# Row maxima and scores of an ALiBi attention: the block bias with its operands swapped, the value matmuls spread evenly, one copy moved from GpSimd to ScalarE

## The chip, the cores and the metric

The kernel runs on one core of one Trainium2 chip. The metric is the device time of one execution in microseconds (us). Three runs of the kernel before gave 3437.27, 3439.45 and 3440.22 us, a median of 3439.45 us.

## What is computed

Four layers run one after another on 8 sequences of 1024 tokens by 256 channels, each as `x = x + layer(layernorm(x))`: a recurrent mixer, a feed-forward layer, attention, and the feed-forward layer again. Only the attention is touched. Its core is:

```python
qkv = (x @ Wqkv + bqkv).reshape(B, L, 3, 16, 16)         # B 8, L 1024
scores = jnp.einsum('bqhd,bkhd->bhqk', q, k) / math.sqrt(16)
bias = -jnp.abs(pos[None, :] - pos[:, None])
scores = scores + slopes[None, :, None, None] * bias[None, None]
probs = jax.nn.softmax(scores, axis=-1)
out = jnp.einsum('bhqk,bkhd->bqhd', probs, v).reshape(B, L, D)
return out @ Wout + bout
```

## The kernel before

The 16 heads of a batch are taken in 4 groups of 4, so attention has 32 groups, numbered 0 to 31. Query and key of a head are stacked in 64 partitions (`q_stack`, `k_stack`): high and low halves of the numbers, and rows that carry the linear part of the ALiBi bias and the shift of the softmax. TensorE's array is used in two row groups of 64, so that two heads' matmuls can run side by side.

A matmul over a stack gives 128 by 512 scores. The stacked rows describe the bias of a block of 128 by 128 on the diagonal only up to a correction. `add_block_bias` adds that correction to the 128 columns of such a block, by two matmuls in bfloat16 that accumulate in PSUM (L1537). Before, a table is the stationary operand (64 partitions by 128 columns) and a 64 by 64 identity, `unit`, is the moving one, so each of the two writes 64 columns.

Scores are computed twice. Once with queries on the partitions, by `find_maxima` (L1593): VectorE reduces each 128 by 512 result to row maxima (L1811), which are transposed on TensorE (L1584), copied by ScalarE (L1723), split by GpSimd into a high part (a copy that rounds, L1903) and the rest (L1905), and taken by DMA through DRAM into a row of `q_stack` (L1988, L1992). And once with keys on the partitions, by `attend` (L1654): ScalarE exponentiates 128 by 1024 scores of two heads (L1762) and TensorE weighs the values with them (`weigh`, L1609), in one PSUM bank that collects 8 key blocks. At the end of 8, ScalarE copies that bank out (L1731, semaphore `pv_made`), the first weighing of the next 8 waits for that copy, and `conclude` transposes the copy (L1621) for VectorE to normalize. For the last group of a batch, `conclude` also has 8 steps of output projection (L1632 to L1641), then the store of the batch and the load of a later one (L2007, L1951).

The order is written out, the same on each engine. A group has two halves (of 512 queries), a half has 8 key blocks `kb`, and a key block has 2 steps, `pair` 0 and 1. A **step** here is one such pair: two `attend` matmuls (one per row group), two `find_maxima` matmuls of the next group or the one after, and a weighing. So a group has 32 steps, attention 1024. In half of the steps the `attend` scores meet the diagonal, in half the maxima do, independently: of 32 steps, 8 have no block bias (plain), 16 have four of its matmuls, and 8 have eight. Row maxima run 80 of their turns ahead (the lead). They use a ring of three PSUM banks, `misc`, which all other short results share. `follow` says which weighing stands at a step's end, and calls `step()`, which takes `conclude` one step further. Other work is laid between by `side_by_side`: queries and keys for a later group (two blocks of 4 matmuls, near steps 2 and 7), values in the last group of a batch, LayerNorm in the second (`normalize`, whose bn_stats is L1782).

Of the kernel before, what the change touches and what calls it, by code (L numbers as in the profile page):

```python
# [7 lines left out]
BF16 = mybir.dt.bfloat16  # L8
# [3 lines left out]
ACT = mybir.ActivationFunctionType  # L12
AX = mybir.AxisListType

P = 128
# [25 lines left out]
GROUPS = HEADS // GROUP  # L41
QB = SEQ // P
# [4 lines left out]
STACK = SHIFTROW + 2  # L47
ROWGROUPS = P // STACK
# [8 lines left out]
def constants():  # L57
    c = {"c_ident": np.eye(P, dtype=np.float32)}

    s, t = np.arange(P)[:, None] % BLOCK, np.arange(BLOCK)[None, :]
    parts = [(s == t) | (s // 2 == t // 2) & (s % 2 == 0) & (t % 2 == 1)]
    for level in range(1, NEARBY):
        m = 1 << level
        parts.append(((s // (2 * m) == t // (2 * m)) & (s // m % 2 == 0))[:, t[0] // m % 2 == 1])
    c["c_mask"] = np.concatenate(parts, 1).astype(np.float32)

    q, power = np.arange(SEQ), np.asarray([power for _, power in slopes()])[:, None, None]
    picked = (q[None, :] // P == np.arange(QB)[:, None]).astype(np.float32)
    i, j = np.arange(QB)[:, None], q[None, :] // P
    sign, near = np.where(i == j, np.where(i < CT, -1, 1), np.sign(i - j)), np.arange(P)
    c["c_qrows"] = np.concatenate([(picked * (q % P))[1:QB - 1], picked])
    c["c_krows"] = np.ones((STACK - SHIFTROW, SEQ))
    c["c_kbias"] = np.concatenate([-power * sign[1:QB - 1], power * (sign * (q % P) - P * np.abs(i - j))], 1)
    short = np.minimum(0, 2 * (near[None, :] - near[:, None]))  # L80
    short = np.stack([short, short.T]).reshape(2, P // STACK, STACK, P)
    by_head = power[:, :, :, None, None] * short
    c["c_block"] = by_head.reshape(GROUPS, ROWGROUPS, GROUP // ROWGROUPS, 2, P // STACK, STACK, P).transpose(
        1, 5, 0, 2, 3, 4, 6).reshape(P, HEADS // ROWGROUPS, 2, P // STACK, P)
    c["c_unit"] = np.tile(np.eye(STACK), (ROWGROUPS, 1))
    c["c_qkscale"] = np.concatenate([np.repeat([HD ** -0.5 / unit for unit, _ in slopes()[:GROUP]], HD),
                                     np.ones(GROUP * HD)])[:, None]
    c = {k: v.astype(np.float32) for k, v in c.items()}
    return {k: np.ascontiguousarray(v) for k, v in c.items()}
# [1292 lines left out]
def attention(nc, banks, x_in, x_out, d):  # L1382
    with nc.cleanup_on_exit(), ExitStack() as ctx:
        sb = lambda n, s, dt=F32: ctx.enter_context(nc.sbuf_tensor("b_" + n, s, dt))
# [6 lines left out]
        PAIRS = GROUP // ROWGROUPS  # L1391
        PARTS = P // STACK
        WIDTH = BANK // 2

        ident, unit = sb("ident", [P, P]), sb("unit", [P, STACK], BF16)
        tables = sb("tables", [P, HEADS // ROWGROUPS, 2, PARTS, P], BF16)
        w_qk = sb("w_qk", [P, KT, GROUPS, 2 * GW])
        w_v, w_out = sb("w_v", [P, KT, DIM]), sb("w_out", [P, KT, DIM])
# [16 lines left out]
        shift, shift_full = sb("shift", [2 * GROUP * QB, P], F32R), sb("shift_full", [2 * GROUP * QB, P])  # L1415
# [14 lines left out]
        ident_in, weights_in, bias_cast, tables_cast = sem("ident_in"), sem("weights_in"), sem("bias_cast"), sem("tables_cast")  # L1430
# [3 lines left out]
        shift_out, shift_in = sem("shift_out"), [sem(f"shift_in{i}") for i in range(2)]  # L1434
# [8 lines left out]
        shift_hi, shift_copied, shift_made = sem("shift_hi"), sem("shift_copied"), sem("shift_made")  # L1443
# [44 lines left out]
        def tails(weigh, conclude):  # L1488

            waiting = []

            def values_of(t, part):
                if t >= 0:
                    use, kb = divmod(t, QB)
                    weigh(t, use, kb, part)
                    if kb == QB - 1 and part:
                        waiting.append(conclude(use // HALVES, use % HALVES))

            def step():
                if waiting and next(waiting[0], waiting) is waiting:
                    waiting.pop(0)

            def follow(t, pair):
                if pair == 0:
                    if (t - 2) % QB == 0:
                        values_of(t - 2, 0)
                    values_of(t - 2, 1)
                elif (t - 1) % QB:  # L1510
                    values_of(t - 1, 0)
                    step()

            def finish():
                end = ALL * HALVES * QB
                values_of(end - 2, 1)
                values_of(end - 1, 0)
                values_of(end - 1, 1)
                while waiting:
                    step()  # L1520

            return follow, finish
# [7 lines left out]

        def tensor(pe):
            def add_block_bias(out, g, pair, rg, variant):

                rows = slice(rg * STACK, (rg + 1) * STACK)
                for part in range(PARTS):
                    cols = slice(part * STACK, (part + 1) * STACK)
                    last = pe.matmul(out[:, cols], tables[rows, g % GROUPS * PAIRS + pair, 1 - variant, part, :], unit[rows, :],  # L1537
                                     start=False, stop=part == PARTS - 1, tile_position=(rg * STACK, 0))
                return last

# [136 lines left out]
        def scalar(act):  # L1677
# [38 lines left out]
            def find_maxima():  # L1716
                for g, turn, *_ in row_turns():
                    if g and turn == TURN + 1:
                        m = misc.at["turn", g - 1][0:2 * GROUP * QB, 0:P]
                        act.wait_ge(max_turned, g)  # L1720
                        if g >= 2:
                            act.wait_ge(shift_made, g - 1)
                        act.activation(shift_full[:, :], m, ACT.Copy).then_inc(shift_copied, 1)  # L1723
                    yield

# [133 lines left out]
        def gpsimd(pool):  # L1859
# [36 lines left out]
            def find_maxima():  # L1896
                lo = slice(0, GROUP * QB)
                for g, turn, *_ in row_turns():
                    if g and turn == TURN + 1:
                        pool.wait_ge(shift_copied, g)  # L1900
                        if g >= 2:
                            pool.wait_ge(shift_out, 16 * (g - 1))
                        pool.tensor_copy(shift[:, :], shift_full[:, :]).then_inc(shift_hi, 1)  # L1903
                        pool.wait_ge(shift_hi, g)
                        pool.tensor_tensor(shift[lo, :], shift_full[lo, :], shift[lo, :].bitcast(F32), ALU.subtract).then_inc(shift_made, 1)  # L1905
                    yield

# [27 lines left out]
            for first in range(0, P, STACK):  # L1935
                pool.dma_start(q_stack[first + MAIN:first + SHIFTROW, :, :], every_slot(d["c_qrows"])).then_inc(tables_cast, 16)
                pool.dma_start(k_stack[first + SHIFTROW:first + STACK, :, :], every_slot(d["c_krows"])).then_inc(tables_cast, 16)
            pool.dma_start(unit[:, :], d["c_unit"]).then_inc(tables_cast, 16)
            pool.dma_start(tables[:, :, :, :, :], d["c_block"]).then_inc(tables_cast, 16)
            pool.wait_ge(half_set, 1)  # L1940
            pool.wait_ge(bias_made, 1)
# [143 lines left out]
```

## Time and profile before

| | |
|---|---|
| median of three runs | 3439.45 us |
| the profiled execution | 3439.45 us, its span 3437.7 us |
| TensorE matmul / weight load, busy in the span | 3188.2 us (93%) / 1915.5 us (56%) |
| VectorE / ScalarE / GpSimd, busy | 2472.0 / 1989.0 / 779.2 us |
| block bias matmuls (L1537) | 4096, mean 197 ns |
| `attend` (L1654) / `find_maxima` (L1593) matmuls | 2048, mean 470 ns / 2048, mean 480 ns |
| row maxima on VectorE (L1811) | 2048, mean 686 ns |
| exponentials on ScalarE (L1762) | 1024, mean 1027 ns |

The 1024 steps take 1766.5 us, from 1289.57 to 3056.1 us of the span; in front of them stand the attention's own beginning and the lead. A length that the profile gives for a matmul includes its way through the array, so two that follow each other overlap in it; what a matmul costs is read from starts. `out<-in` names the tiles, and `x16` after a row of the timeline says that so many instructions were put together. A matmul on f32 appears as two instructions.

### The profile page before, as it was taken

To read this page: it belongs to the slowest core of one execution; us is meant where nothing else is said; L and a number is where in the kernel's file an instruction comes from. 1 tells how busy PE (TensorE), PEld (TensorE's weight loads), DVE (VectorE), ACT (ScalarE), POOL (GpSimd) and SP (SyncE) were. 2 spreads that over 40 slices of the span, in tenths; PEclk is the share of its full clock that TensorE was granted. 3 is DMA by queue.
4 is the path that set the end of the run, shared out by engine and by line. 5 is a ranking of instruction groups with operands and counts; after the bars stand their busy time and mean duration, and the time that the engine had idled before them with its cause. 6 is when DMAs were issued, how large, how long until landed. Compare 5 with 4: busy or idle time off the path is not lost. (4 is left out here: it accounts for less than half of the span.)

```text
span 3437.7 us, 77976 instructions
## 1 busy us (share of the span) xinstructions
PE 3188.2 (93%) x31396; PEld 1915.5 (56%) x31396; DVE 2472.0 (72%) x4742; ACT 1989.0 (58%) x2967; POOL 779.2 (23%) x920
## 2 busy tenths in 40 slices
PE   7999999977999479999999999999999999979998
PEld 3666666655777334454444544544445445437777
DVE  6877777737777258877778777787787777817776
ACT  3544445534555207666667666666676676765555
POOL 3444444432222201011021020110201201012222
PEclk9999999977999759999999999999999999989999
DMA  1000000002111322122222131222221312111110
GB/s 52 15 26 27 26 21 27 20 28 93 50 50 38 90 43 38 31 44 48 44 48 44 24 68 24 44 49 45 47 45 26 66 30 39 36 57 51 53 53 32
DMA packets 110295, 145.44 MB, mean 42 GB/s; under 512 B 21744, under 2 KB 94208, under 8 KB 109152
## 3 DMA queue, kind: packets, MB, share of 16 engines
q1 hardware_dynamic: 109168, 137.69, 17.1%
q8 instruction: 249, 4.08, 0.5%
q0 software_dynamic: 768, 2.77, 0.4%
q14 instruction: 110, 0.90, 0.1%
HBM read 53.79 MB, written 38.24 MB: 27 GB/s over the span
## 5 line engine op out<-in xcount | busy, mean ns | idle before, releaser
L1811 DVE TENSOR_REDUCE b_half_max<-banks 128x1 f32<-128x512 f32 x2048 | 1310.1, 686 | 423.2 <-PE banks L1537 273.1
L1762 ACT ACTIVATE b_p_t<-banks 128x1024 f32<-128x1024 f32 x1024 | 1040.7, 1027 | 366.5 <-PE banks L1537 234.5
L1593 PE MATMUL banks<-b_k_stack,b_q_stack 62*128 62x512 f32 x2048 | 827.6, 480 | 43.5 <-issue 17.8
L1654 PE MATMUL banks<-b_q_stack,b_k_stack 64*128 64x512 f32 x2048 | 833.2, 470 | 8.1 <-ACT b_p_t L1762 8.0
L1609 PE MATMUL banks<-b_p_t,b_v 128*17 128x256 f32 x8192 | 631.8, 386 | 0.2 <-ACT b_p_t L1762 0.2
L1654 PEld LDWEIGHTS banks<-b_q_stack,b_k_stack 64*128 64x128 f32 x2048 | 345.4, 186 | 421.9 <-issue 371.5
L1593 PEld LDWEIGHTS banks<-b_k_stack,b_q_stack 62*128 62x128 f32 x2048 | 339.2, 189 | 91.2 <-DVE b_half_max L1811 41.7
L1537 PE MATMUL banks<-b_unit,b_tables 64*128 64x64 bf16 x4096 | 371.3, 197 | 0.0
L1137 ACT ACTIVATE ffn_relu<-banks,ffn_scale_fc 128x512 f32<-128x512 f32 x256 | 176.2, 688 | 234.0 <-PE banks L1069 234.0
L1082 PE MATMUL banks<-ffn_proj_t,ffn_r_hi 128*128 128x256 f32 x1024 | 262.1, 289 | 9.0 <-DVE ffn_r_lo L1263 9.0
L1083 PE MATMUL banks<-ffn_proj_t,ffn_r_lo 128*128 128x256 f32 x1024 | 253.4, 280 | 0.0
L1537 PEld LDWEIGHTS banks<-b_unit,b_tables 64*128 64x128 bf16 x4096 | 185.2, 97 | 121.2 <-issue 73.1
L1609 PEld LDWEIGHTS banks<-b_p_t,b_v 128*17 128x17 f32 x8192 | 142.9, 95 | 173.2 <-ACT b_p_t L1762 50.7
L1261 DVE CAST ffn_r_hi<-ffn_square 128x512 fp32r<-128x512 f32 x256 | 129.2, 505 | 142.3 <-ACT ffn_square L1141 140.6
L1893 POOL TENSOR_TENSOR b_qk_lo<-b_qk,b_qk_hi 128x512 fp32r<-128x512 f32 x64 | 81.8, 1278 | 628.9 <-ACT b_qk L1712 474.2
L1082 PEld LDWEIGHTS banks<-ffn_proj_t,ffn_r_hi 128*128 128x128 f32 x1024 | 194.5, 190 | 24.6 <-DVE ffn_r_lo L1263 15.1
L1065 PE MATMUL banks<-ffn_x_hi,ffn_fc_t 128*128 128x512 f32 x512 | 203.3, 397 | 0.0
L1066 PE MATMUL banks<-ffn_x_lo,ffn_fc_t 128*128 128x512 f32 x512 | 202.7, 396 | 0.0
L1319 POOL TENSOR_TENSOR ffn_x<-ffn_x,ffn_scaled_out 128x256 f32<-128x256 f32 x128 | 108.2, 845 | 402.8 <-DVE ffn_scaled_out L1274 402.8
L1083 PEld LDWEIGHTS banks<-ffn_proj_t,ffn_r_lo 128*128 128x128 f32 x1024 | 193.4, 189 | 8.3
L1263 DVE TENSOR_TENSOR ffn_r_lo<-ffn_square,ffn_r_hi 128x512 fp32r<-128x512 f32 x256 | 177.3, 693 | 8.8
L1141 ACT ACTIVATE ffn_square<-ffn_relu 128x512 f32<-128x512 f32 x256 | 162.0, 633 | 8.2
(232 smaller groups left out, 4722.6 us busy)
## 6 DMA issues: line engine op xcount, KB each, us to landing
ffn_x<-x SPq DMA_DIRECT2D x32, 512.0 KB, 3.8
b_q_stack<-b_qk_hi SPq DMA_DIRECT2D x256, 64.0 KB
b_k_stack<-b_qk_hi SPq DMA_DIRECT2D x256, 64.0 KB
a_x<-hidden_states SPq DMA_DIRECT2D x16, 512.0 KB, 4.1
x<-a_x SPq DMA_DIRECT2D x16, 512.0 KB, 2.9
x<-ffn_x SPq DMA_DIRECT2D x16, 512.0 KB, 2.8
b_x<-x SPq DMA_DIRECT2D x8, 1024.0 KB, 5.5
b_k_stack<-b_qk_lo SPq DMA_DIRECT2D x128, 64.0 KB
```

Of the source, the lines that this page charges most:

```text
L1065: pe.matmul(b, fc_t[:, kt, cols], x_hi[:, kt, :], start=kt == 0, stop=False)
L1066: pe.matmul(b, fc_t[:, kt, cols], x_lo[:, kt, :], start=False, stop=False)
L1082: pe.matmul(b[:, 0:DIM], r_hi[par][:, m, i * P:(i + 1) * P], proj_t[:, m, :], start=m == 0, stop=False)
L1083: last = pe.matmul(b[:, 0:DIM], r_lo[par][:, m, i * P:(i + 1) * P], proj_t[:, m, :], start=False, stop=m == HT - 1)
L1137: act.activation(relu[use % 2][:, :], high[use % 3], ACT.Relu, scale=scale_fc[:, m:m + 1]).then_inc(relu_made, 1)
L1263: dve.tensor_tensor(r_lo[par][:, m, :], square[use % 2][:, :], r_hi[par][:, m, :].bitcast(F32), ALU.subtract).then_inc(r_lo_made, 1)
L1537: last = pe.matmul(out[:, cols], tables[rows, g % GROUPS * PAIRS + pair, 1 - variant, part, :], unit[rows, :], start=False, stop=part == P ...
L1593: last = pe.matmul(m, q_stack[rows, slot, qb * P:(qb + 1) * P], k_stack[rows, slot, half * BANK:(half + 1) * BANK], start=True, stop=not h ...
L1609: last = pe.matmul(values[i * SLOT:i * SLOT + VW, cols], v[:, kb, hg * GROUP + i, :], p_t[(2 * t + i % 2) % P_BUFS][:, i // 2, cols], star ...
L1654: last = pe.matmul(out, k_stack[stack, slot, kb * P:(kb + 1) * P], q_stack[stack, slot, half * BANK:(half + 1) * BANK], start=True, stop=n ...
L1762: act.activation(p_t[use % P_BUFS][:, :, :], scores[use % 2], ACT.Exp, scale=slopes()[pair][0]).then_inc(p_made, 1)
L1811: dve.tensor_reduce(half_max[:, (pair + rg * PAIRS) * QB + qb, half:half + 1], misc.at["max", g, turn], axis=AX.X, op=ALU.max, negate=True ...
```

## The change

Four things change.

- The two block bias matmuls swap their operands. `halves` (a 128 by 128 identity cut into two parts of 64 rows) is stationary and the table is moving, so each writes all 128 columns.
- `follow` puts one weighing at the end of every step. Before, the first weighing of a half was put off, so that one step had none and the next had two. `step()` is now called in each second step; before, it was left out at the first one of a half.
- ScalarE writes the rounded high part of the maxima itself, from PSUM, ahead of the full copy. GpSimd's copy goes. ScalarE waits for the DMA that reads the last high part (`shift_out`) where it waited for GpSimd.
- The constant that is loaded for it is 128 by 2 by 128 in place of 128 by 64.

```diff
-    c["c_unit"] = np.tile(np.eye(STACK), (ROWGROUPS, 1))
+    c["c_halves"] = np.tile(np.eye(P).reshape(P // STACK, STACK, P).transpose(1, 0, 2), (ROWGROUPS, 1, 1))
...
             def follow(t, pair):
                 if pair == 0:
-                    if (t - 2) % QB == 0:
-                        values_of(t - 2, 0)
                     values_of(t - 2, 1)
-                elif (t - 1) % QB:
+                else:
                     values_of(t - 1, 0)
                     step()
...
                 for part in range(PARTS):
-                    cols = slice(part * STACK, (part + 1) * STACK)
-                    last = pe.matmul(out[:, cols], tables[rows, g % GROUPS * PAIRS + pair, 1 - variant, part, :], unit[rows, :],
+                    last = pe.matmul(out, halves[rows, part, :], tables[rows, g % GROUPS * PAIRS + pair, variant, part, :],
                                      start=False, stop=part == PARTS - 1, tile_position=(rg * STACK, 0))
...
                         if g >= 2:
-                            act.wait_ge(shift_made, g - 1)
+                            act.wait_ge(shift_out, 16 * (g - 1))
+                        act.activation(shift[:, :], m, ACT.Copy).then_inc(shift_hi, 1)
                         act.activation(shift_full[:, :], m, ACT.Copy).then_inc(shift_copied, 1)
...
+                        pool.wait_ge(shift_hi, g)
                         pool.wait_ge(shift_copied, g)
-                        if g >= 2:
-                            pool.wait_ge(shift_out, 16 * (g - 1))
-                        pool.tensor_copy(shift[:, :], shift_full[:, :]).then_inc(shift_hi, 1)
-                        pool.wait_ge(shift_hi, g)
                         pool.tensor_tensor(shift[lo, :], shift_full[lo, :], shift[lo, :].bitcast(F32), ALU.subtract).then_inc(shift_made, 1)
```

On TensorE, at the beginning of a second half, before (L1654 attend, L1593 maxima, L1537 block bias, L1609 weighing, L1621 transposes of the collected values; the first row is key block 1, pair 1):

```order
L1654 MATMUL banks<-b_q_stack,b_k_stack 128x512
L1593 MATMUL banks<-b_k_stack,b_q_stack 128x512
L1537 MATMUL banks<-b_unit,b_tables 128x64 x2
L1654 MATMUL banks<-b_q_stack,b_k_stack 128x512
L1593 MATMUL banks<-b_k_stack,b_q_stack 128x512
L1537 MATMUL banks<-b_unit,b_tables 128x64 x2
L1654 MATMUL banks<-b_q_stack,b_k_stack 128x512
L1593 MATMUL banks<-b_k_stack,b_q_stack 128x512
L1654 MATMUL banks<-b_q_stack,b_k_stack 128x512
L1593 MATMUL banks<-b_k_stack,b_q_stack 128x512
L1609 MATMUL banks<-b_p_t,b_v 17x256 x8
```

The same place in the changed kernel, from key block 1, pair 1 (the lines are five lower):

```order
L1649 MATMUL banks<-b_q_stack,b_k_stack 128x512
L1588 MATMUL banks<-b_k_stack,b_q_stack 128x512
L1532 MATMUL banks<-b_tables,b_halves 128x128 x2
L1649 MATMUL banks<-b_q_stack,b_k_stack 128x512
L1588 MATMUL banks<-b_k_stack,b_q_stack 128x512
L1532 MATMUL banks<-b_tables,b_halves 128x128 x2
L1604 MATMUL banks<-b_p_t,b_v 17x256 x4
L1616 MATMUL banks<-b_ident,b_pv 128x128 x4
```

A weighing and the four transposes now stand in the first of the two steps, and the bias matmuls are 128 columns wide; before, the transposes stood a step after the double weighing.

On SyncE, in a first group of a batch, before (L1988 and L1992 carry the maxima out and back in, L2007 stores a batch, L1951 loads one):

```order
L1977 DMA b_k_stack<-b_k_bias 14x1024
L1988 DMA b_shift_dram1<-b_shift 64x128
L1992 DMA b_q_stack<-b_shift_dram1 2x2048 x2
L2007 DMA x2<-b_x0 128x8x256
L1951 DMA b_x0<-x1 128x8x256
```

And in the changed kernel:

```order
L1970 DMA b_k_stack<-b_k_bias 14x1024
L2000 DMA x2<-b_x0 128x8x256
L1944 DMA b_x0<-x1 128x8x256
L1981 DMA b_shift_dram1<-b_shift 64x128
L1985 DMA b_q_stack<-b_shift_dram1 2x2048 x2
```

The store and the load of a batch now stand ahead of that group's maxima, two key blocks earlier.

## Rows read from the trace of the kernel before

**Rows 1.** Windows, all attention steps: stretch, length, busy us by engine, PEclk, DMA share, GB/s
```profile
1289.57:3056.10 1766.53, 1727.62 (x17382) 864.34 (x17380) 1330.90 (x2239) 1223.37 (x1433) 226.71 (x311) 0.99 0.21 41
```
**Rows 2.** Timeline of TensorE, a plain and a four-bias step: start us, length us, instruction
```profile
1649.68 0.50 PE L1654 MATMUL banks<-b_q_stack,b_k_stack 64*128 64x512 f32 x1
...
1650.90 0.49 PE L1654 MATMUL banks<-b_q_stack,b_k_stack 64*128 64x512 f32 x1
...
1652.28 0.49 PE L1654 MATMUL banks<-b_q_stack,b_k_stack 64*128 64x512 f32 x1
```
**Rows 3.** Timeline of TensorE, an eight-bias step
```profile
2012.90 0.50 PE L1654 MATMUL banks<-b_q_stack,b_k_stack 64*128 64x512 f32 x1
...
2013.25 0.23 PE L1537 MATMUL banks<-b_unit,b_tables 64*128 64x64 bf16 x4
...
2013.64 0.23 PE L1537 MATMUL banks<-b_unit,b_tables 64*128 64x64 bf16 x4
2013.81 0.63 PE L1609 MATMUL banks<-b_p_t,b_v 128*17 128x256 f32 x8
2014.36 0.50 PE L1654 MATMUL banks<-b_q_stack,b_k_stack 64*128 64x512 f32 x1
```
**Rows 4.** Timeline of TensorE's weight loads, the same step
```profile
2013.29 0.19 PEld L1593 LDWEIGHTS banks<-b_k_stack,b_q_stack 62*128 62x128 f32 x1
```
**Rows 5.** Timeline of TensorE, beginning of a first half in group 6
```profile
1629.01 0.50 PE L1654 MATMUL banks<-b_q_stack,b_k_stack 64*128 64x512 f32 x1
...
1630.48 0.49 PE L1654 MATMUL banks<-b_q_stack,b_k_stack 64*128 64x512 f32 x1 [0.34 <-ACT b_p_t L1762]
...
1630.81 0.20 PE L1537 MATMUL banks<-b_unit,b_tables 64*128 64x64 bf16 x1
...
1630.85 0.19 PE L1537 MATMUL banks<-b_unit,b_tables 64*128 64x64 bf16 x1
...
1632.28 0.49 PE L1654 MATMUL banks<-b_q_stack,b_k_stack 64*128 64x512 f32 x1
...
1634.31 0.50 PE L1654 MATMUL banks<-b_q_stack,b_k_stack 64*128 64x512 f32 x1
```
**Rows 6.** Timeline of ScalarE, the same stretch
```profile
1630.31 0.61 ACT L1731 ACTIVATE b_pv<-banks 128x512 f32<-128x512 f32 x1
```
**Rows 7.** Timeline of TensorE, beginning of a second half in group 6
```profile
1653.50 0.49 PE L1654 MATMUL banks<-b_q_stack,b_k_stack 64*128 64x512 f32 x1
...
1656.27 0.50 PE L1654 MATMUL banks<-b_q_stack,b_k_stack 64*128 64x512 f32 x1
...
1658.24 0.50 PE L1654 MATMUL banks<-b_q_stack,b_k_stack 64*128 64x512 f32 x1
```
**Rows 8.** Timeline of ScalarE, the same stretch
```profile
1653.97 0.59 ACT L1731 ACTIVATE b_pv<-banks 128x512 f32<-128x512 f32 x1
```
**Rows 9.** Waits of VectorE, 1300 to 2900 us: total us, times, longest us
```profile
DVE b_stats L1782 <- DMA b_x<-x: 11.2, 6, 2.7
```
**Rows 10.** Timeline of GpSimd, end of a batch's output
```profile
2460.38 0.72 POOL L1921 TENSOR_TENSOR b_x<-b_x,b_b_out 128x256 f32<-128x256 f32 x1
```
**Rows 11.** Timeline of SyncE's DMA issues, the same batch
```profile
2466.42 0.39 SPq L2007 DMA_DIRECT2D x<-b_x  x1
2472.77 0.38 SPq L1951 DMA_DIRECT2D b_x<-x  x1
```
**Rows 12.** Timeline of TensorE, the LayerNorm that follows
```profile
2482.29 0.50 PE L1593 MATMUL banks<-b_k_stack,b_q_stack 62*128 62x512 f32 x1 [3.23 <-DVE b_half_max L1811]
```
**Rows 13.** Busy time by engine, 3.4 us behind that wait
```profile
2483.60:2487.00 3.40, 3.40 (x28) 1.26 (x27) 1.79 (x3) 1.74 (x2) 2.73 (x4) 0.50 0.02 5
```
**Rows 14.** Timeline of ScalarE, the transposed maxima in group 6
```profile
1664.70 0.26 ACT L1723 ACTIVATE b_shift_full<-banks 64x128 f32<-64x128 f32 x1
```
**Rows 15.** Timeline of TensorE, the same stretch
```profile
1665.02 0.50 PE L1593 MATMUL banks<-b_k_stack,b_q_stack 62*128 62x512 f32 x1 [0.28 <-ACT b_shift_full L1723]
```
**Rows 16.** Busy time by engine, the lead, when row maxima run alone
```profile
1220.00:1289.00 69.00, 64.35 (x201) 31.93 (x201) 47.74 (x79) 6.28 (x13) 3.28 (x4) 0.57 0.19 33
```

More of the change, by code:

```diff
@@ L1393, in attention @@
         WIDTH = BANK // 2
-        ident, unit = sb("ident", [P, P]), sb("unit", [P, STACK], BF16)
+        ident, halves = sb("ident", [P, P]), sb("halves", [P, PARTS, P], BF16)
         tables = sb("tables", [P, HEADS // ROWGROUPS, 2, PARTS, P], BF16)
@@ L1937, in gpsimd @@
                 pool.dma_start(k_stack[first + SHIFTROW:first + STACK, :, :], every_slot(d["c_krows"])).then_inc(tables_cast, 16)
-            pool.dma_start(unit[:, :], d["c_unit"]).then_inc(tables_cast, 16)
+            pool.dma_start(halves[:, :, :], d["c_halves"]).then_inc(tables_cast, 16)
             pool.dma_start(tables[:, :, :, :, :], d["c_block"]).then_inc(tables_cast, 16)
```

## The prediction

> **What bounds the kernel now.** I read the busy times by stretch first, then the timeline of TensorE step by step, then the waits. Over the attention's 1024 steps TensorE has a matmul in flight for 1727.6 of 1766.5 us at a granted clock of 0.99 of 2.4 GHz; VectorE is busy for 1330.9 and ScalarE for 1223.4 us [rows 1]. So a step is as long as TensorE's own work, except where a wait interrupts it. Clean steps, from start to start of the first L1654: plain 1650.90 - 1649.68 = 1.22 us, four-bias 1652.28 - 1650.90 = 1.38 [rows 2], eight-bias 2014.36 - 2012.90 = 1.46 [rows 3]. Each ends with a weighing of 2014.36 - 2013.81 = 0.55. The reader should see that the waits on the chain are few and always the same, at a half's beginning, at the transposed maxima and at a LayerNorm. The sum is made against the profiled execution: span 3437.7 us, time 3439.45, 1.75 us around the span; that is also the median.
>
> **The change, part by part.**
>
> *Wider block bias.* Two bias matmuls of a row group start 0.04 us apart (1630.81, 1630.85) [rows 5]: 64 columns at 2.4 GHz are 0.027, the rest is getting the weights in. 64 more columns add 0.027 to each, side by side in the two row groups. What of it shows depends on what follows. After the first of a pair comes the second: shown. After the second of the first pair comes the next 512-column matmul. Its weights begin to load at 2013.29 [rows 4], just as that second bias matmul starts (2013.25 + 0.04), and from there to the next bias at 2013.64 it is 0.35 [rows 3], as long as the step's first scores matmul needs (2013.25 - 2012.90 = 0.35) with its weight load wholly in the open. So the load already outlasts the bias matmul; 0.35 - 0.213 (512 columns) = 0.137 covers 0.054 of columns, and the growth is hidden. After the second of the last pair comes the weighing on all rows, which needs the array empty: shown. An eight-bias step grows by 3 x 0.027 = 0.080. In a four-bias step a row group has one pair, and the last one lies in the shadow of the other group's late 512-column matmul: 0.027. A group grows by 8 x 0.080 + 16 x 0.027 = 1.07 us. About 30.75 groups have both kinds of scores (the last group has no maxima beside it and goes at the exponentials' pace): 33.0 us. Bounds: only the last growth of an eight-bias step shows, 8 x 0.027 x 30.75 = 6.6; all of it shows, (8 x 0.107 + 16 x 0.053) x 30.75 = 52.4. A gain is excluded, as count and loads stay. I take 33, since the loads' starts bear it out.
>
> The Trainium skill (TensorE: Matmul & The Clock Gate, Back-to-back issue gap) gives about 60 cycles to a matmul of 1 to 64 columns and 134 to one of 128. By that, an estimate, a bias matmul grows by 74 cycles or 0.031 us, and with none hidden this term would be 61, not 33. Its Part 3 (What overlaps and what doesn't) says weights load beside a matmul only in another row group; this speaks for none hidden, but the trace shows the load of the same row group starting with the bias matmul [rows 4].
>
> *Even weighings, first half of a group.* The first weighing of a half needs ScalarE's copy L1731, and now stands in the step in which that copy runs. There the copy ends at 1630.31 + 0.61 = 1630.92 [rows 6], 1.91 after the step's start at 1629.01 [rows 5], because ScalarE first empties the query and key blocks. Before, that weighing stood a step later and waited for nothing. Now: weighing at 1.91 + 0.06 hand-over = 1.97; + 0.55; + the four transposes, 1634.31 - 1632.28 = 2.03 less 1.46 = 0.57 [rows 5]; then a four-bias step 1.38 + 0.03 and an eight-bias one 1.46 + 0.08. Together 6.04 against 1634.31 - 1629.01 = 5.30 before [rows 5]. Of the 0.74, 0.19 is wider bias, counted above: 0.55. This holds at 22 beginnings (31 that have such a copy, less 2 last groups without query and key blocks, less 7 at a LayerNorm, where the wait falls into VectorE's and I count nothing): 12.1 us.
>
> *Second half.* The copy ends at 1653.97 + 0.59 = 1654.56 [rows 8], 1.06 after 1653.50 [rows 7]. Now 1.12 + 0.55 + 0.57 + 1.22 + 1.41 = 4.87, before 1658.24 - 1653.50 = 4.74: 0.13, less 0.05 of bias, 0.08 x 31 = 2.5. Before, the light and the heavy step took 1656.27 - 1653.50 = 2.77 together [rows 7], where two clean ones are 1.38 + 1.22 = 2.60: the light one outran VectorE. That stall goes and one for the copy comes. The last two groups and the first half of all: 1.3 by the same working.
>
> *Store and load of a batch.* They move ahead of the maxima's DMAs on SyncE. A batch is ready at 2460.38 + 0.72 [rows 10], yet its store is issued at 2466.42 and the load at 2472.77 [rows 11]: behind the maxima. VectorE then waits for it, 11.2 us in 6 times [rows 9], TensorE behind VectorE up to 3.23 [rows 12]. After four of the six, the granted clock is 0.50 for 3.4 us [rows 13], 1.7 lost each. Now the store can go at about 2457 (last tile a key block or two earlier, nothing in front), the load some 9 us earlier, and the longest wait is 2.7: all gone, -(11.2 + 6.8) = -18.0. The price: SyncE is held by the store, and the maxima's two small DMAs share the queues with 1 MB of load; they are needed at the next group's start, a quarter of a group later. Nothing counted; bounds 0 and 7 times 2.7 us, the longest that the load itself was late.
>
> *The moved copy.* TensorE's ring waits for ScalarE's copy at 1664.70 + 0.26 and resumes at 1665.02 [rows 14, 15]. ScalarE now does two of these before the bank is free: + 0.20 (0.26 less the overlap of neighbours; bounds 0.1 and 0.26) x 31 = 6.2. GpSimd's saved copy gives nothing: nobody waited for it.
>
> *The lead.* 80 maxima in 69 us at a clock of 0.57 [rows 16]; 20 pairs of bias at half clock, 0.08 each: 1.6. The larger constant is loaded long before the first maximum: 0.
>
> Sum: 33.0 + 12.1 + 2.5 + 1.3 - 18.0 + 6.2 + 1.6 = 38.7. 3439.45 + 38.7 = 3478.
>
> **The rivals.**
>
> - *All columns show.* For it: one row group's matmuls are strictly in turn. Against: rows 4. 33.0 becomes 52.4: 3498.
> - *Hardly any shows*, because waits for ScalarE and VectorE take it in. For it: VectorE's 1330.9 us are 1.30 a step, above a plain step. Against: four-bias steps do differ from plain ones now. 6.6 for 33.0: 3452.
> - *The load gains nothing*, because what it saves comes back as late maxima at the next group's start. 3478 + 18 = 3496.
> - *Waits lower the clock.* The new wait in the first half is 1.97 - 0.99 = about 1 us, 22 times, with a short one soon behind. If each costs 3.4 us at half clock: 22 x 1.7 = 37, 3515. Against: the wait there now (1630.48 less 1629.01 + 0.91) is 0.56 and the granted clock over all steps 0.99; 3.23 costs clock.
> - *Faster: the copy isn't late.* If ScalarE's copy were out before TensorE reaches the weighing, 0.99 after the step's start (not 1.97), the first halves would give 0.24 each and the second ones 0.13: -5.3 - 4.0 in place of + 14.6. With hardly any column shown: 6.6 - 9.3 - 18.0 + 6.2 = -14.5, 3425. Its place is the weighing at key block 1, pair 1. Against: ScalarE's order there is unchanged, and it is busy through.
>
> **How the numbers follow.** Forecast 3478 with 0.50; all shown 0.14; hardly any 0.13; load without gain 0.09; clock 0.07; faster 0.07. A time within 0.2% (3432.6 to 3446.3) can't be told from no change. Slower by more takes the first five but the low tail of "hardly any": 0.88; the same 0.05; faster 0.07. The range leaves out the faster case, part of "hardly any" and the clock: 3453 to 3503.
>
> **What would show it.** Bias matmuls in the same number, 4096; eight-bias steps of about 1.54 us, four-bias 1.41, plain 1.22. In a group's first half the weighing at key block 1, pair 1 waits for L1727 (the copy's new line) about 1 us, in the second half 0.25. VectorE no longer waits for b_x, and no clock of 0.5 is left between 1340 and 3050 us. The bank of the transposed maxima is free 0.2 later. I am wrong if four-bias steps keep 1.38 or reach 1.43, if the copy ends earlier in its step, or if the LayerNorm groups stay as long as they are.

## The result, and the profile of the changed kernel

The changed kernel takes 3479.5 us (median of four runs, 3478.15 to 3480.33), the kernel before, beside it, 3439.8. The ratio is 1.011, with a 95% interval of 1.0091 to 1.013: slower by some 40 us, where the prediction said 3478. The profiled execution took 3481.96 us with a span of 3480.2. The steps, from the start of the first L1649 to the last, take 1806.3 us against 1766.5. That is 39.8 more, of the 42.5 by which the two profiled spans differ (3480.2 against 3437.7). Nearly the whole loss lies in the steps: the first one starts 2.4 later than before, and the part behind the last step is as long as it was (381.9 against 381.5).

The rows that answer to [rows 1 to 3], first the windows over nearly all steps (columns as in [rows 1]):

```profile
1340.00:3050.00 1710.00, 1664.90 (x16413) 818.33 (x16413) 1289.47 (x2167) 1158.43 (x1384) 214.09 (x276) 1.00 0.21 41
```

The granted clock is 1.00 over the stretch. The four half-clock stretches of before, one of which is [rows 13], are gone. The bias matmuls in the page (line, engine, operation, tiles, shapes, count, then busy us and mean ns):

```profile
L1532 PE MATMUL banks<-b_tables,b_halves 64*128 64x128 bf16 x4096 | 435.8, 223 | 0.0
```

Their number is the same, their mean length 223 ns against 197. TensorE's timeline in group 6, a plain and a four-bias step of the second half; a step runs from one row shown to the next:

```profile
1659.01 0.50 PE L1649 MATMUL banks<-b_q_stack,b_k_stack 64*128 64x512 f32 x1
...
1660.24 0.49 PE L1649 MATMUL banks<-b_q_stack,b_k_stack 64*128 64x512 f32 x1
...
1661.64 0.49 PE L1649 MATMUL banks<-b_q_stack,b_k_stack 64*128 64x512 f32 x1
```

Plain is 1660.24 - 1659.01 = 1.23 us, four-bias 1661.64 - 1660.24 = 1.40. The beginning of the same group's first half, to be laid beside [rows 5]:

```profile
1637.51 0.50 PE L1649 MATMUL banks<-b_q_stack,b_k_stack 64*128 64x512 f32 x1
...
1639.40 0.63 PE L1604 MATMUL banks<-b_p_t,b_v 128*17 128x256 f32 x8 [0.78 <-ACT b_pv L1727]
...
1640.54 0.50 PE L1649 MATMUL banks<-b_q_stack,b_k_stack 64*128 64x512 f32 x1
...
1641.95 0.49 PE L1649 MATMUL banks<-b_q_stack,b_k_stack 64*128 64x512 f32 x1
...
1643.48 0.50 PE L1649 MATMUL banks<-b_q_stack,b_k_stack 64*128 64x512 f32 x1
```

And ScalarE there, answering to [rows 6]:

```profile
1638.74 0.60 ACT L1727 ACTIVATE b_pv<-banks 128x512 f32<-128x512 f32 x1
```

The copy ends at 1639.34, 1.83 us after the step's start, and the weighing follows 0.06 later, after a wait of 0.78 (about 1 was predicted). The three steps take 1643.48 - 1637.51 = 5.97, where they took 5.30. The last of them is an eight-bias step, 1.53. The second half's beginning, beside [rows 7]:

```profile
1662.86 0.49 PE L1649 MATMUL banks<-b_q_stack,b_k_stack 64*128 64x512 f32 x1
...
1663.98 0.63 PE L1604 MATMUL banks<-b_p_t,b_v 128*17 128x256 f32 x8 [0.20 <-ACT b_pv L1727]
...
1667.74 0.50 PE L1649 MATMUL banks<-b_q_stack,b_k_stack 64*128 64x512 f32 x1
```

Three steps in 4.88, before 4.74. The place of [rows 14, 15] on ScalarE, then on TensorE:

```profile
1674.38 0.26 ACT L1718 ACTIVATE b_shift<-banks 64x128 fp32r<-64x128 f32 x1
1674.53 0.27 ACT L1719 ACTIVATE b_shift_full<-banks 64x128 f32<-64x128 f32 x1
```

```profile
1674.85 0.50 PE L1588 MATMUL banks<-b_k_stack,b_q_stack 62*128 62x512 f32 x1 [0.45 <-ACT b_shift_full L1719]
```

The two copies take 1674.80 - 1674.38 = 0.42 us where one took 0.26, and TensorE waits 0.45 for them in place of 0.28. The waits of the whole engine list, 1300 to 2950 us (columns as in [rows 9]), hold a new one for `b_pv` and none for `b_x`. The one for `b_shift_full` was there before, with 6.4 us in 22 places:

```profile
PE banks L1604 <- ACT b_pv L1727: 22.2, 50, 0.8
PE banks L1588 <- ACT b_shift_full L1719: 9.5, 21, 0.5
```

Last, SyncE's issues for the batch of [rows 11]:

```profile
2485.75 0.39 SPq L2000 DMA_DIRECT2D x<-b_x  x1
2491.50 0.38 SPq L1944 DMA_DIRECT2D b_x<-x  x1
2494.48 0.48 SPq L1981 DMA_DIRECT2D b_shift_dram<-b_shift  x1
2497.43 0.55 SPq L1985 DMA_DIRECT2D b_q_stack<-b_shift_dram  x2
```

Store and load stand ahead of the maxima. They no longer wait for them.

### The profile page after: what moved, and what is told of

Read it like the earlier page. It is cut to its first block and busy times, and to the rows that moved or that the text cites. A ratio compares the mean times of both kernels' runs of the same rounds, so it can differ in the third digit from the quotient of the medians.

```text
span 3480.2 us, 77977 instructions
## 1 busy us (share of the span) xinstructions
PE 3223.5 (93%) x31396; PEld 1914.4 (55%) x31396; DVE 2473.6 (71%) x4742; ACT 1998.0 (57%) x2999; POOL 768.7 (22%) x888
## 5 line engine op out<-in xcount | busy, mean ns | idle before, releaser
L1649 PE MATMUL banks<-b_q_stack,b_k_stack 64*128 64x512 f32 x2048 | 851.6, 469 | 0.0
L1604 PE MATMUL banks<-b_p_t,b_v 128*17 128x256 f32 x8192 | 640.9, 385 | 25.1 <-ACT b_pv L1727 24.5
L1649 PEld LDWEIGHTS banks<-b_q_stack,b_k_stack 64*128 64x128 f32 x2048 | 342.9, 185 | 432.3 <-issue 416.8
L1532 PE MATMUL banks<-b_tables,b_halves 64*128 64x128 bf16 x4096 | 435.8, 223 | 0.0
L1604 PEld LDWEIGHTS banks<-b_p_t,b_v 128*17 128x17 f32 x8192 | 135.9, 95 | 225.3 <-issue 77.3
L1532 PEld LDWEIGHTS banks<-b_tables,b_halves 64*128 64x128 bf16 x4096 | 185.0, 96 | 117.1 <-issue 57.3
```

Source lines behind the costliest of these rows:

```text
L1532: last = pe.matmul(out, halves[rows, part, :], tables[rows, g % GROUPS * PAIRS + pair, variant, part, :], start=False, stop=part == PARTS ...
L1604: last = pe.matmul(values[i * SLOT:i * SLOT + VW, cols], v[:, kb, hg * GROUP + i, :], p_t[(2 * t + i % 2) % P_BUFS][:, i // 2, cols], star ...
L1649: last = pe.matmul(out, k_stack[stack, slot, kb * P:(kb + 1) * P], q_stack[stack, slot, half * BANK:(half + 1) * BANK], start=True, stop=n ...
```

## The ledger by groups

A group's length is the time from its first `attend` matmul to that of the next group. The 31 groups before the last fall into four kinds, by their place in a batch of four: the first (index 0), the one with LayerNorm (1), a quiet one (2) and the one with values (3). Sums of each kind in us, from each kernel's profiled execution. The experiments are told of below.

| kernel | first (8) | LayerNorm (8) | quiet (8) | values (7) | all steps |
|---|---|---|---|---|---|
| before | 479.3 | 443.3 | 398.6 | 412.1 | 1766.5 |
| changed | 493.0 | 437.6 | 412.9 | 427.7 | 1806.3 |
| e1, wide bias alone | 486.4 | 443.5 | 406.7 | 419.2 | 1789.8 |
| e2, second of a pair wide | 479.4 | 443.0 | 400.7 | 413.9 | 1770.6 |
| e3, first of a pair wide | 484.9 | 443.4 | 404.6 | 417.6 | 1784.0 |
| e5, even weighings alone | 484.3 | 428.8 | 404.2 | 419.8 | 1771.5 |
| e6, even weighings, late store | 484.7 | 457.5 | 404.2 | 419.9 | 1800.6 |
| e7, moved copy alone | 480.4 | 443.9 | 399.7 | 413.2 | 1770.4 |
| e4, store early | 491.1 | 433.1 | 399.0 | 411.9 | 1768.3 |
| e8, changed, late store | 492.5 | 451.1 | 412.9 | 427.8 | 1819.4 |
| e9, store early, load behind maxima | 479.7 | 425.9 | 398.8 | 412.2 | 1749.8 |
| e10, maxima copied a turn earlier | 472.9 | 422.3 | 393.1 | 406.7 | 1728.1 |

In the 23 groups without LayerNorm, the three parts alone give 22.3 + 18.3 + 3.3 = 43.9 us, all together 43.6: there they add. In the eight LayerNorm groups the change gains 5.7. If the bias and the copy cost as much there as elsewhere, 0.97 a group (22.3 / 23) and 0.14 (3.3 / 23), they cost 7.8 + 1.1, and with e5's gain of 14.5 that makes a gain of 5.6, beside the 5.7 measured. How e5's 14.5 divides isn't measured by itself: e9 gains 17.4 there without the even weighings, so 2.9 is put down to the weighings and 17.4 to the store and load. By this estimate 5.7 + 7.8 + 1.1 + 2.9 = 17.5 us came back.

## The experiments

Each is timed against the kernel before on the same chip, whose median was 3443 to 3447 us in these rounds. Times are medians, and ratios carry their 95% interval.

### e1: the wide bias alone

```diff
-                    last = pe.matmul(out[:, cols], tables[rows, g % GROUPS * PAIRS + pair, 1 - variant, part, :], unit[rows, :],
+                    last = pe.matmul(out, halves[rows, part, :], tables[rows, g % GROUPS * PAIRS + pair, variant, part, :],
```

> The kernel before with the swapped, 128-column block bias alone. Theory (the second of a pair is hidden behind the next weight load): four-bias steps 1.40 us, eight-bias 1.53, and the step at key block 1 with the queries and keys between its pairs 3.58 instead of 3.48, as both pairs are followed by something that needs them done; 33 + 2.5 + 1.6 = +37 us, 3477. Rival (all columns show): four-bias 1.43, eight-bias 1.56, +52 or more, 3492.

Measured: 3471.2 us, ratio 1.008 (1.0068 to 1.0093). Group 6 of its timeline, a four-bias step and a plain one, then an eight-bias one:

```profile
1654.51 0.50 PE L1653 MATMUL banks<-b_q_stack,b_k_stack 64*128 64x512 f32 x1
...
1655.91 0.50 PE L1653 MATMUL banks<-b_q_stack,b_k_stack 64*128 64x512 f32 x1
...
1657.13 0.50 PE L1653 MATMUL banks<-b_q_stack,b_k_stack 64*128 64x512 f32 x1
...
1678.30 0.50 PE L1653 MATMUL banks<-b_q_stack,b_k_stack 64*128 64x512 f32 x1
...
1679.82 0.49 PE L1653 MATMUL banks<-b_q_stack,b_k_stack 64*128 64x512 f32 x1
```

Four-bias 1.40, plain 1.22, eight-bias 1.52. The rows show hundredths, so the medians over all steps of groups 0 to 30 that have no other work in them say more: four-bias 1.374 before and 1.400 in e1 (289 steps), eight-bias 1.452 and 1.532 (145 steps). These are the growths that the prediction gave, 0.027 and 0.080. Group 6 grew by 1.03 (1.07 predicted). The steps grew by 23.3 only, where 37 was expected for the time and some 26 to 28 came, since the LayerNorm groups did not grow (443.5). There the late load hid it: while VectorE's wait for `b_x` fell from 11.2 to 6.7 us and the half-clock stretches from four to two, TensorE's longer steps filled the time.

```profile
DVE b_stats L1781 <- DMA b_x<-x: 6.7, 6, 1.9
```

### e2 and e3: only the second, only the first bias matmul of a pair wide

```diff
+                    cols, wide = slice(part * STACK, (part + 1) * STACK), part == 1      # e3: part == 0
+                    last = pe.matmul(out if wide else out[:, cols], tables[rows, g % GROUPS * PAIRS + pair, 1 - variant, part, :],
+                                     halves[rows, part, :] if wide else halves[rows, part, cols],
```

> The kernel before; only the second bias matmul of each pair writes 128 columns (its moving operand is the identity padded with zeros, the sum is unchanged). Theory: the first pair's second one hides behind the next weight load, so four-bias steps stay at 1.38, eight-bias steps go from 1.455 to 1.48; +7 to +9 us, 3448. Rival (each column shows wherever it stands): half of the wide bias, four-bias 1.39 to 1.40, +17 to +26 us, 3457 to 3466.

> The kernel before; only the first bias matmul of each pair writes 128 columns. Theory: it is always followed by its partner, so it always shows: four-bias steps 1.40, eight-bias 1.51; +27 to +30 us, 3468. Rival (each column shows alike): the same time as with the second one wide, 3457 to 3466.

Measured: e2 3452.1, ratio 1.0029 (1.0016 to 1.0042); e3 3463.3, 1.0067 (1.005 to 1.0084). The times by themselves don't decide: e2's is nearer to the 3448 of the theory than to the rival's 3457, but e3's stayed below its 3468 and inside the rival's range, as in e1 because the LayerNorm groups did not grow. The steps decide. Group 6 grew by 0.27 in e2 and by 0.76 in e3, together the 1.03 of e1. In the 23 groups without LayerNorm it was 4.0 and 17.1 us. The tables stay stationary in both, so the growth is that of the columns, and of the 22.3 us of e1 at most 1.2 are left for the swap itself. The eight-bias step of e2, then of e3, on TensorE:

```profile
1671.25 0.50 PE L1655 MATMUL banks<-b_q_stack,b_k_stack 64*128 64x512 f32 x1
...
1672.72 0.49 PE L1655 MATMUL banks<-b_q_stack,b_k_stack 64*128 64x512 f32 x1
```

```profile
1677.76 0.50 PE L1655 MATMUL banks<-b_q_stack,b_k_stack 64*128 64x512 f32 x1
...
1679.26 0.49 PE L1655 MATMUL banks<-b_q_stack,b_k_stack 64*128 64x512 f32 x1
```

The two steps are 1.47 and 1.50, from 1.45 to 1.46 before. By the medians, eight-bias steps grew from 1.452 to 1.479 and 1.507, and four-bias steps from 1.374 to 1.373 in e2, that is not at all, and to 1.401 in e3. The same number of columns was added in both, 2048 matmuls by 64, and only the place in the pair differs. In these steps a first bias matmul always shows its columns, with the second one behind it. A second shows them where the weighing comes next. Where a 512-column matmul comes next, that one's weights load meanwhile, as TensorE's weight loads of e2 show in the step above:

```profile
1671.63 0.19 PEld L1594 LDWEIGHTS banks<-b_k_stack,b_q_stack 62*128 62x128 f32 x1
```

The load begins as the widened second matmul starts, 0.04 after the first at 1671.59. This is the step of the prediction that put the term at 33 and not at 52.4. The rule of the Trainium skill (TensorE: Matmul & The Clock Gate, What overlaps and what doesn't) that weights load beside a matmul only in another row group would have e2 and e3 cost the same, and the measurement goes against it: 0.27 against 0.76.

### e4: the store of a batch issued two calls earlier

```diff
-                for _ in range(QB):
+                for _ in range(QB - 2):
```

(in SyncE's `conclude`, with nothing else changed.)

> The kernel before; on SyncE alone a batch's store and the load behind it stand two key blocks earlier, ahead of the maxima's DMAs; nothing else moves. Theory: VectorE's waits for b_x (11.2 us, 6 times) go, and with them the stretches at a granted clock of 0.5 between 1340 and 3050 us: -18 to -20 us, 3420. Rival (the gain comes back as late maxima at the start of the next group, or the clock falls elsewhere): -5 to +3 us, 3435 to 3443.

Measured: 3447.9, ratio 1.001 (1.0 to 1.002): no gain. My theory was that going ahead of the maxima frees the load and costs nothing, and it fell here. SyncE's issues at one batch:

```profile
2240.73 0.39 SPq L2007 DMA_DIRECT2D x<-b_x  x1
2246.03 0.38 SPq L1951 DMA_DIRECT2D b_x<-x  x1
2246.51 0.64 SPq L1988 DMA_DIRECT2D b_shift_dram<-b_shift  x1
2251.74 0.56 SPq L1992 DMA_DIRECT2D b_q_stack<-b_shift_dram  x2
```

From the maxima's way out to their way in are 5.2 us behind 1 MB of load. At the batch of [rows 11] of the kernel before, with neither store nor load ahead of them, it was 2465.85 - 2464.05 = 1.8:

```profile
2464.05 0.48 SPq L1988 DMA_DIRECT2D b_shift_dram<-b_shift  x1
2465.85 0.53 SPq L1992 DMA_DIRECT2D b_q_stack<-b_shift_dram  x2
```

The maxima are needed at the next group's start, and TensorE waits for them. Its list of waits, then the start itself and the stretch behind:

```profile
PE banks L1654 <- DMA b_q_stack<-b_shift_dram: 11.2, 6, 2.7
```

```profile
2254.02 0.79 PE L1654 MATMUL banks<-b_q_stack,b_k_stack 64*128 64x512 f32 x1 [2.10 <-DMA b_q_stack<-b_shift_dram]
```

```profile
2254.00:2264.00 10.00, 9.98 (x46) 4.17 (x46) 6.60 (x21) 2.37 (x3) 1.67 (x3) 0.50 0.01 2
```

The LayerNorm groups gave back 10.2 us, and the first groups took 11.8. This is the rival "the load gains nothing", in the kernel before. Why it is not so in the changed kernel is seen in e5.

### e5: the even weighings alone

```diff
                 if pair == 0:
-                    if (t - 2) % QB == 0:
-                        values_of(t - 2, 0)
                     values_of(t - 2, 1)
-                elif (t - 1) % QB:
+                else:
```

> The kernel before with one weighing at the end of every step, and the step of the output each second step, on all engines; bias and copy as before. Theory: first halves +0.55 us at 22 places, second halves +0.08 at 31, the last groups 1.3, and the earlier store and load -18 to -20: -2 to -4 us, 3436. Rival (evening out removes TensorE's waits): -20 us or more, 3420. Rival (the weighing's wait costs clock): +20 or more, 3460.

Measured: 3449.9, ratio 1.0002 (0.9984 to 1.002). The time can't be told from no change, and the steps take 5.0 us more, where 2 to 4 less were expected. The 23 groups without LayerNorm lose 18.3, the LayerNorm groups gain 14.5, and 1.2 falls on the last group. No wait for `b_x` is left and no half clock. The new wait on TensorE:

```profile
PE banks L1607 <- ACT b_pv L1729: 24.8, 51, 0.8
```

Evenly called, `step()` reaches the batch's last tile earlier, and the store follows. In e4 SyncE's turn was moved but the output was not, so SyncE stood waiting for GpSimd's last tile with the maxima queued behind. SyncE's waits for it, in e4 and in the changed kernel:

```profile
SPq L2007 <- POOL b_x L1921: 71.3, 7, 10.9
```

```profile
SPq L2000 <- POOL b_x L1914: 28.6, 7, 4.6
```

What matters more is how far the load is ahead of the maxima: 0.5 us in e4 (2246.03, 2246.51), 3.0 in the changed kernel (2491.50, 2494.48), where the maxima go out and in within 2.9 us. At the six batches with a load they have landed 2.7 to 3.6 us before the next group begins. In e4 that group begins only as they land.

### e6 and e8: the store put back behind the maxima

```diff
-                for _ in range(QB):
+                for _ in range(QB + 2):
```

(e6 with the even weighings alone, e8 in the changed kernel.)

> As the even weighings alone, but SyncE's store and load kept where they were, behind the maxima's DMAs. Theory: the even weighings without their side effect: +16 us, 3455, with VectorE's waits for b_x back (6 times). Rival (the store's place does nothing): same as the even weighings alone, 3436.

> The changed kernel with SyncE's store and load put back behind the maxima's DMAs. Theory: 3479.5 plus what the early store gained, 10 to 20 us: 3490 to 3500, with waits for b_x. Since the steps are longer, the load may be less late than it was. Rival (the store's place does nothing): 3479.

Measured: e6 3479.0, ratio 1.0091 (1.0066 to 1.0115), 31 us above e5 by the ratios. e8 3504.4, a little above the 3490 to 3500 expected, ratio 1.0157 (1.013 to 1.0184), 16 us above the changed kernel by the ratios (0.0047 of 3440). The waits for the load came back, in e6 and in e8:

```profile
DVE b_stats L1780 <- DMA b_x<-x: 15.4, 6, 3.0
```

```profile
DVE b_stats L1778 <- DMA b_x<-x: 8.2, 6, 2.2
```

Nothing but the place of the store and the load differs, so the order on SyncE is the cause of the gain. The size in e6 was missed: I had put it 16 us above the kernel before and it was 31. The LayerNorm groups went from 428.8 to 457.5, more than before's 443.3, with half clock at each of the six waits (3.4 us once, 6.8 five times). In e8 the term is 13.5 in those groups, with two such stretches of 6.8. So its size depends on how late the load is and on how often the clock falls.

### e7: the moved copy alone

```diff
+                        act.activation(shift[:, :], m, ACT.Copy).then_inc(shift_hi, 1)
                         act.activation(shift_full[:, :], m, ACT.Copy).then_inc(shift_copied, 1)
...
-                        pool.tensor_copy(shift[:, :], shift_full[:, :]).then_inc(shift_hi, 1)
```

> The kernel before with the high part of the maxima written by ScalarE, GpSimd's copy gone. Theory: the bank of the transposed maxima is free 0.16 us later, 31 times: +5 to +6 us, 3445. Rival (the shorter path through GpSimd pays, or nothing waits for the bank): 0, 3440.

Measured: 3449.0, ratio 1.0003 (0.9986 to 1.002). The steps take 3.9 us more, and group 6 grows by 0.13. The step behind the transposes went from 2.23 to 2.39 us, as ScalarE's 0.16 says. The ratio alone can't tell this from nothing.

### e9: the store early and the load behind the maxima

```diff
-                for _ in range(QB):
+                for _ in range(QB - 1):
                     yield
                 sp.wait_ge(y_biased, QB * (b + 1))
                 sp.dma_start(...)                      # the store
+                yield
                 load(b + 2)
```

> The kernel before; on SyncE a batch's store stands one key block earlier, ahead of the maxima's DMAs, and the load stays behind them. Nothing else moves. Theory (in the early-store run the 1 MB load stood in the queues ahead of the maxima, which landed when the next group began): the store goes about 5 us earlier, the load about 6 us, VectorE's waits for b_x (2.7 at most) go and TensorE doesn't wait for the maxima's DMAs: 61.1 us in first groups of a batch, 53.6 in second ones, -17 us against the kernel before. Rival (SyncE's wait for the batch alone delays the maxima): first groups 62 or more, no gain.

Measured: 3423.7, ratio 0.9945 (0.9928 to 0.9963). SyncE at the batch of [rows 11]:

```profile
2453.98 0.39 SPq L2007 DMA_DIRECT2D x<-b_x  x1
2456.89 0.48 SPq L1988 DMA_DIRECT2D b_shift_dram<-b_shift  x1
2458.71 0.53 SPq L1992 DMA_DIRECT2D b_q_stack<-b_shift_dram  x2
2459.29 0.38 SPq L1951 DMA_DIRECT2D b_x<-x  x1
```

The maxima go out and in within 1.8 us again at this batch and three others. At the other three it took 2.4 to 3.3. The first groups keep their length, and the LayerNorm groups lose 17.4, without a wait for `b_x` and without half clock. So the waits and the clock together are worth about what the prediction had put on them (18.0), and e4 lost it to the order of load and maxima.

### e10: ScalarE copies the transposed maxima one turn earlier

```diff
-                    if g and turn == TURN + 1:
+                    if g and turn == TURN:
```

> The kernel before; ScalarE's copy of the transposed maxima stands one turn earlier in its order, ahead of the step's exponential instead of behind it. Theory: TensorE's wait for that bank (0.77 us in the step behind, 31 times) is ScalarE's order, not its speed: that step falls from 2.23 to about 1.46, -20 to -24 us. Rival (the copy then waits for the transpose and delays the exponential, which TensorE needs two steps later): 0 to -8 us.

Measured: 3404.2, ratio 0.9888 (0.9874 to 0.9903), some 39 us less, where 20 to 24 were expected. In the kernel before, TensorE made the transpose at 1662.71, finished that step and went into the next, while the copy stood a step later on ScalarE, behind an exponential, and ended at 1664.96 ([rows 14]). TensorE of before around it:

```profile
1662.71 0.30 PE L1584 MATMUL banks<-b_ident,b_row_max 128*64 128x128 f32 x1
...
1664.23 0.50 PE L1654 MATMUL banks<-b_q_stack,b_k_stack 64*128 64x512 f32 x1
...
1666.46 0.50 PE L1654 MATMUL banks<-b_q_stack,b_k_stack 64*128 64x512 f32 x1
```

In e10, on TensorE and then on ScalarE, the copy follows its transpose at once:

```profile
1664.64 0.30 PE L1584 MATMUL banks<-b_ident,b_row_max 128*64 128x128 f32 x1
...
1666.16 0.50 PE L1654 MATMUL banks<-b_q_stack,b_k_stack 64*128 64x512 f32 x1
...
1667.62 0.50 PE L1654 MATMUL banks<-b_q_stack,b_k_stack 64*128 64x512 f32 x1
```

```profile
1664.97 0.27 ACT L1723 ACTIVATE b_shift_full<-banks 64x128 f32<-64x128 f32 x1 [0.18 <-PE banks L1584]
```

The step behind the transposes falls from 1666.46 - 1664.23 = 2.23 to 1667.62 - 1666.16 = 1.46 us, the length of a clean eight-bias step. The groups without LayerNorm gain 17.3, 0.75 each. The LayerNorm groups gain 21.0, of which 6 are the same 0.75, and 15 came unforeseen. The maxima's DMAs, and the store and the load behind them, are issued earlier (the load 0.8 to 2.3 us, measured to the next group's start). Of the waits for `b_x` 2.2 us are left of 11.2, and none of the four half-clock stretches, by the prediction's prices 9.0 + 6.8 = 15.8:

```profile
DVE b_stats L1782 <- DMA b_x<-x: 2.2, 4, 0.6
```

### e11 and e12: e9 and e10 together; e10's edit in the changed kernel

> The split store and the earlier copy together, on the kernel before. Theory: they add up, -37 to -41 us, about 1.1% below the kernel before. Rival: the shorter groups bring the waits for b_x back, and half of the sum is left, -20.

> The changed kernel; ScalarE's two copies of the transposed maxima stand one turn earlier, ahead of the step's exponential. Theory: what the moved copy costs and what was there before it go together: the step behind falls from 2.48 to 1.53, -25 to -29 us against the changed kernel, 10 above the kernel before. Rival: two copies ahead of the exponential delay it, and TensorE waits for it: -10 at most.

Measured: e11 3402.9, ratio 0.9882 (0.9869 to 0.9894), steps 1726.1. e11 is 20 us faster than e9 but can't be told from e10, whose interval overlaps with its own. It adds 2 us of steps to e10, not e9's 17, because e10 had already taken most of the same waits away. So the expected 37 to 41 us came, but not as the sum of two effects: e10 brings nearly all of it alone. e12 3456.6, ratio 1.0039 (1.0027 to 1.0051), steps 1777.6, 28.7 below the changed kernel. The step behind the transposes went from 2.48 to 1.54 there, as expected. The changed kernel so mended is still slower than before.

## Why the prediction was right, by its own steps

- **What bounds it** held. TensorE is busy for 1664.9 of 1710 us at full clock, and each term shows in the starts of its steps.
- **Wider bias, 33.0.** About 30 by an estimate from e1: 22.3 us in 23 groups is 0.97 a group, times 30.75 (e1 itself shows 23.3, with none in the LayerNorm groups). The sizes of the steps held (1.40 and 1.53 against 1.41 and 1.54), and e2 and e3 show the reason held too. Two places were mis-sized. A four-bias step with query and key blocks between its two pairs grew by 0.11 in e1 (3.48 to 3.58), not 0.027: both its pairs are followed by something that needs them done. And where TensorE waits for ScalarE, the columns vanish in the wait: the eight-bias step that begins at 1629.01 in [rows 5] ends in a wait of 0.34 for an exponential, which is 0.28 in e1, and the step is 0.05 shorter there, not 0.08 longer. The step behind the transposes, with its wait of 0.28, did grow by 0.08. The gap that the Trainium skill gives (TensorE: Matmul & The Clock Gate, Back-to-back issue gap) would have made the term 61, an estimate, if no column were hidden. e2 rules out that none is; where the columns show, a matmul grew by 0.026 to 0.028, beside the 0.031 of that gap.
- **Even weighings, 12.1 + 2.5 + 1.3 = 15.9.** The mechanism held in the rows: the three steps of a first half take 5.97 where 6.04 was predicted, those of a second half 4.88 for 4.87. The copy ends 1.83 after the step's start for 1.91, and 1.06 for 1.06. The size was low: 18.3 in 23 groups, 2.9 in the LayerNorm groups (by the division above), 1.2 in the last, together 22.4. By itself (e5) a first half costs 0.57 in quiet groups (0.62 in group 6), not 0.55, a second half 0.12, not 0.08, since the bias, taken off these sums in full, was partly hidden in the wait. The groups with values cost 1.1 each (7.7 / 7), where 0.63 was counted: 0.80 at the first half's beginning and 0.32 at the second's. There the third of the three steps gives back 0.4 us, where it gives back 0.6 in a quiet group; why stays open. And a LayerNorm group, counted with its second half alone, cost 0.36 (2.9 / 8).
- **Store and load, -18.0.** -17.4 in e9 and, by the estimate that uses it, -17.5 in the changed kernel. Put back there, the store and load cost 13 to 16 (e8), and beside the even weighings alone 29 to 31 (e6), so the size holds for one kernel at a time. The price counted at nothing was nothing here, but not in general: in e4 the same order cost 11.8 in the first groups, because the batch was not ready earlier and the load went out right ahead of the maxima.
- **The moved copy, 6.2.** Measured 3.9 in e7 and 0.14 a group, for 0.20. The two copies overlap more than was taken.
- **The lead, 1.6.** It can't be told: from the first maxima matmul to the first step are 67.5 to 72.2 us in the kernels of this study, whether the bias is wide in them or not.
- **The rivals.** "All columns show" would have made e2 as dear as e3, and it was not. "Hardly any" is refuted by 22.3 us. "Waits lower the clock" did not come: waits of up to 0.8 for the copy in 50 places, and the clock granted is 1.00 over the stretch. "The copy isn't late" is refuted by the copy's end at 1.83. "The load gains nothing" was true of e4 and false here.

The terms as measured sum to 30 + 22.4 - 17.5 + 4 = 39, beside 39.8 in the steps and 38.7 predicted. That it came so close is partly luck, by errors that cancel: weighings 6.5 too low, bias, copy and lead together 6 to 7 too high.

## What to carry to other kernels

Before an operand swap, write out what follows each matmul in its row group: here the added columns cost where another short matmul or one on the whole array came next, and not where a weight load already took longer. A copy that frees a ring of banks should stand in the order right behind what it copies; here one turn took 38.4 us off the steps, about as much as the four parts of the change together added (39.8). When a large and a small transfer share a queue, put the small one that someone waits for ahead of the large one.

## What the runs showed of the hardware that was not expected

- Small transfers behind 1 MB on one queue: from the maxima's way out to their way in took 5.2 us where 1 MB of load had been issued 0.5 before (e4), 2.9 where it had been issued 3.0 before (the changed kernel), and 1.8 without it.
- Half clock goes with TensorE's long pauses. Between 1340 and 3040 us, in the fourteen profiles of this study, it had 28 pauses of 2.1 to 3.5 us without a matmul in flight, and a stretch at a granted 0.50, 1.2 GHz, stands at 25 of them; of 19 pauses of 1.0 to 1.5 us, at three. The 50 waits of at most 0.8 us in the changed kernel brought none. A stretch lasted 3.4 us, or two or three times that.
- Weights for the same row group load while a bfloat16 matmul of 128 columns runs, so that its last 64 columns cost nothing (e2: four-bias steps 1.373 for 1.374).
